# Ordering the experts of a mixture layer one step deeper and splitting the first half of the down product into three float32r matmuls

## What is computed

```
E, F, D, C = 64, 256, 512, 117          # experts, hidden width, token width, capacity of an expert
hg = einsum('ecd,efd->ecf', expert_in, w_gate)      # expert_in: the tokens routed to the expert, 117 slots
hu = einsum('ecd,efd->ecf', expert_in, w_up)
expert_out = einsum('ecf,edf->ecd', silu(hg) * hu, w_down)
sparse = segment_sum(gate * expert_out, token)      # each token chose 6 experts
```

## Time and profile before

| | before |
|---|---|
| median of 3 runs | 990.45 us (990.37 to 992.57) |
| the profiled execution, own time | 991.27 us |
| its span, first to last instruction | 989.4 us |
| TensorE busy | 912.4 us, 92% |
| VectorE, ScalarE, GpSimd busy | 71%, 45%, 38% |
| mean granted TensorE clock | 0.978 |
| moved by DMA | 159.73 MB |

### The profile page before, as it was taken

The page is one execution under the profiler, slowest core; times in us unless marked ns, Lnnn a source line. Parts: engine busy times, 40 slices in busy tenths (PEclk is TensorE's granted clock), DMA queues, the critical chain, the costliest instruction groups (busy, mean ns, idle before and its releaser), DMA issues. The chain is left out here.

```text
span 989.4 us, 13105 instructions
## 1 busy us (share of the span) xinstructions
PE 912.4 (92%) x4281; PEld 666.8 (67%) x4281; DVE 707.1 (71%) x1315; ACT 445.3 (45%) x696; POOL 380.6 (38%) x326
## 2 busy tenths in 40 slices
PE   5998999979999999989999989799999999999970
PEld 3997544448887778867788777566666666666640
DVE  6856789966654676777767888588677766677765
ACT  2665000052634535435264244566565666666630
POOL 2003000016600454105531153667766666766630
PEclk9999999979999999999999999999999999999995
DMA  6433000033200222012110263599999999999868
GB/s 176 145 121 122 18 1 0 0 117 128 86 1 7 89 86 86 1 54 85 52 61 11 74 224 128 161 331 325 339 340 354 349 329 355 357 356 325 285 176 204
DMA packets 57161, 159.73 MB, mean 161 GB/s; under 512 B 13901, under 2 KB 21651, under 8 KB 48656
## 3 DMA queue, kind: packets, MB, share of 16 engines
q1 hardware_dynamic: 44725, 147.50, 43.4%
q0 software_dynamic: 12288, 11.36, 4.2%
q10 hardware_dynamic: 91, 0.13, 0.1%
HBM read 152.71 MB, written 25.58 MB: 180 GB/s over the span
## 5 line engine op out<-in xcount | busy, mean ns | idle before, releaser
L259 PE MATMUL ps<-split_operands 128*125 128x512 f32 (+5 forms) x690 | 266.2, 386 | 16.2 <-DVE split_operands L1256 5.4
L260 PE MATMUL ps<-split_operands 128*125 128x512 f32 (+5 forms) x690 | 260.4, 377 | 0.0
L261 PE MATMUL ps<-split_operands 128*125 128x512 f32 (+5 forms) x690 | 260.1, 377 | 0.0
L653 POOL DMA_INDIRECT yrow_scratch<-work,row_i x64 | 151.6, 2369 | 95.4 <-ACT work L953 92.8
L259 PEld LDWEIGHTS ps<-split_operands 128*125 128x125 f32 (+3 forms) x690 | 129.5, 188 | 45.3 <-issue 9.6
L1470 DVE TENSOR_TENSOR gate_up_lo<-expert_weights,split_operands 128x2048 fp32r<-128x2048 f32 x64 | 147.0, 2297 | 0.5 <-ACT split_operands L935 0.5
L261 PEld LDWEIGHTS ps<-split_operands 128*125 128x125 f32 (+3 forms) x690 | 129.5, 188 | 26.5
L391 POOL TENSOR_TENSOR split_operands<-work,split_operands 128x512 fp32r<-128x512 f32 x66 | 83.5, 1293 | 162.0 <-ACT split_operands L373 153.1
L260 PEld LDWEIGHTS ps<-split_operands 128*125 128x125 f32 (+3 forms) x690 | 129.6, 188 | 23.6
L935 ACT ACTIVATE split_operands<-expert_weights 128x2048 fp32r<-128x2048 f32 x64 | 121.8, 1903 | 0.0
L1963 PE MATMUL ps<-expert_weights,work 128*117 128x512 f32 x256 | 120.3, 592 | 0.5 <-issue 0.5
(11 more groups left out here) (217 smaller groups left out, 1242.5 us busy)
## 6 DMA issues: line engine op xcount, KB each, us to landing
expert_weights<-experts_in SPq DMA_DIRECT2D x64, 1024.0 KB
expert_weights<-experts_in SPq DMA_DIRECT2D x64, 512.0 KB
work<-w_in SPq DMA_DIRECT2D x12, 1024.0 KB, 5.1
yrow_scratch<-work SPq DMA_DIRECT2D x5, 1500.0 KB
split_operands<-yrow_scratch SPq DMA_DIRECT2D x4, 1120.0 KB
work<-cw_in SPq DMA_DIRECT2D x3, 1024.0 KB, 5.2
work<-rows_in SPq DMA_DIRECT2D x10, 256.0 KB, 4.6
work<-wmix_in SPq DMA_DIRECT2D x4, 512.0 KB, 5.4
```

The source lines that it names most:

```text
L259: pe.matmul(o, a[1], b[0], start=start, stop=False)
L260: pe.matmul(o, a[0], b[1], start=False, stop=False)
L261: return pe.matmul(o, a[0], b[0], start=False, stop=stop)
L653: pool.indirect_dma_start(yrow, bass.IndirectOffsetOnAxis(ap=row_i[:, e:e + 1], axis=0), OS[e % 4], None, bounds_check=last_row, oob_is_er ...
```

## The change

The order on TensorE becomes gate_up(e), transpose_h(e - 1), transpose_x(e + 2), down(e - 2). The first half of the down product (the first 128 of 256 hidden values) becomes three float32r matmuls. So its weights need a high and a low part (`down_hi` on ScalarE and `down_lo` on VectorE, 128x512 each), and so do the turned hidden values (`h_part_hi` on ScalarE; in `h_part_lo` on VectorE a subtraction of 128x117 and a copy of 128x117 stand where one copy of 128x234 stood). The second half stays one plain float32 matmul. scale and with it scatter go one step later (scale(e - 2)). add_choice(0) goes behind the loop. Both engines' lists keep their other operations.

```diff
+        DN_hi = [rg(o, 512) for o in (16272, 32144)]
+        DN_lo = [sb(f"down_lo{r}", [P, 512], F32R, at=rg_at + 4 * (o + WA)) for r, o in enumerate(ring_at)]
...
+        HTP = sb("hidden_pairs", [P, 8 * CAP], F32R, at=fg_at + 4 * 4416)
+        HTR = [(HTP[:, cut(4 * CAP * i, 2 * CAP)], HTP[:, cut(4 * CAP * i + 2 * CAP, 2 * CAP)]) for i in range(2)]
...
+        def halves_done(e, down):
+
+            if down:
+                return len(plan) + min(2 * e + 4, E + e + 1)
+            return len(plan) + max(2 * e - 1, e + 1 if e < 2 else 0)
...
+            def down_hi(e):
+                act.wait_ge(S(f"load_in{RINGS + e % RINGS}"), 16 * (e // RINGS) + 16)
+                if e >= 2:
+                    act.wait_ge(S("o_ps"), e - 1)
+                act.activation(DN_hi[e % 2], RING[e % RINGS][:, cut(WA, 512)], ACT.Copy).then_inc(S("weight_hi"), 1)
+
+            def h_part_hi(e):
+                act.wait_ge(S("ht_ps"), NSH + e + 1)
+                if e >= 2:
+                    act.wait_ge(S("o_ps"), e - 1)
+                act.activation(HTR[e % 2][0][:, 0:CAP], ps[:, 4 + e % 2, 0:CAP], ACT.Copy).then_inc(S("ht_hi"), 1)
...
             for e in range(E):
                 silu(e)
+                if e >= 1:
+                    h_part_hi(e - 1)
                 if e + 2 < E:
                     gate_up_hi(e + 2)
-                if e >= 1:
-                    scale(e - 1)
+                if e >= 2:
+                    scale(e - 2)
+                down_hi(e)
                 if e + 2 < E:
                     xe_hi(e + 2)
+            h_part_hi(E - 1)
+            scale(E - 2)
             scale(E - 1)
...
-                dve.wait_ge(S("weight_hi"), len(plan) + e + 1)
+                dve.wait_ge(S("weight_hi"), halves_done(e, False))
...
-                dve.wait_ge(S("ht_ps"), NSH + e + 1)
+
+            def down_lo(e):
+                dve.wait_ge(S("weight_hi"), halves_done(e, True))
+                dve.tensor_tensor(DN_lo[e % RINGS][:], RING[e % RINGS][:, cut(WA, 512)], f(DN_hi[e % 2]), ALU.subtract).then_inc(S("weight_lo"), 1)
+
+            def h_part_lo(e):
+                dve.wait_ge(S("ht_hi"), NT * NL + e + 1)
                 if e >= 2:
                     dve.wait_ge(S("o_ps"), e - 1)
-                dve.tensor_copy(HTF[e % 2], ps[:, 4 + e % 2, 0:2 * CAP]).then_inc(S("ht_sb"), 1)
+                dve.tensor_copy(HTF[e % 2][:, CAP:2 * CAP], ps[:, 4 + e % 2, CAP:2 * CAP])
+                dve.tensor_tensor(HTR[e % 2][1][:, 0:CAP], ps[:, 4 + e % 2, 0:CAP], f(HTR[e % 2][0][:, 0:CAP]),
+                                  ALU.subtract).then_inc(S("ht_sb"), 1)
...
             for e in range(E):
                 gated(e)
+                if e >= 1:
+                    h_part_lo(e - 1)
                 if e + 2 < E:
                     gate_up_lo(e + 2)
+                down_lo(e)
+                if e + 2 < E:
                     xe_lo(e + 2)
+                if e == E - 1:
+                    h_part_lo(e)
                 if 2 <= e < 4 + TOPK:
                     gates(e - 2)
-                if e == E - 2:
-                    dve.wait_ge(S("shared_add"), NSH)
-                    add_choice(0)
-            for k in range(1, TOPK - 1):
+            dve.wait_ge(S("shared_add"), NSH)
+            for k in range(TOPK - 1):
                 add_choice(k)
...
-                for k in range(2):
-                    last = pe.matmul(ps[0:CAP, 6 + e % 2, :], HTF[e % 2][:, cut(k * CAP, CAP)], RING[e % RINGS][:, cut(WA + 512 * k, 512)],
-                                     start=(k == 0), stop=(k == 1))
+                pe.wait_ge(S("weight_lo"), halves_done(e, True))
+                mm3(ps[0:CAP, 6 + e % 2, :], sub(HTR[e % 2], A_, cut(0, CAP)), (DN_hi[e % 2], DN_lo[e % RINGS][:]), True, False)
+                last = pe.matmul(ps[0:CAP, 6 + e % 2, :], HTF[e % 2][:, CAP:2 * CAP], RING[e % RINGS][:, cut(WA + 512, 512)],
+                                 start=False, stop=True)
                 last.then_inc(S("o_ps"), 1)
...
             for e in range(E):
                 gate_up(e)
                 if e >= 1:
-                    down(e - 1)
-                transpose_h(e)
+                    transpose_h(e - 1)
                 if e + 2 < E:
                     transpose_x(e + 2)
+                if e >= 2:
+                    down(e - 2)
+            transpose_h(E - 1)
+            down(E - 2)
             down(E - 1)
```

More of the change, by code:

```diff
@@ L1948, in gate_up @@
             def gate_up(e):
-                pe.wait_ge(S("weight_lo"), len(plan) + e + 1)
+                pe.wait_ge(S("weight_lo"), halves_done(e, False))
                 pe.wait_ge(S("xe_lo"), e + 1)
```

## The result

The changed kernel takes 1003.75 us in the median of 20 runs (995.06 to 1010.14), the kernel before 997.65 on the same chip (20 runs, 989.39 to 1002.85). The ratio is 1.0067 with a 95% interval of 1.0041 to 1.0093: 0.7% slower, where 0.6% faster was forecast. (It is taken over the comparable runs and not from the two medians, which give 1.0061.) The profiled execution took 1008.2 with a span of 1005.4; the earlier trace rows are from one of 991.27.

The account below looks back on a forecast made before the run. TensorE, busy 92% of the span, was taken as the bound, with transfers next. Terms -9.9 - 0.8 + 0.4 + 1.0 + 3.5 = -5.8 us took the profiled 991.27 to 985.5, median 984.6 (0.6% less), range 981 to 990.

Parts of the forecast that it names:

- The step, -9.9: TensorE's loop step: three float32r matmuls replace one float32, 5.10 becomes 4.93 us over some 60 steps, -9.9 us.
- ScalarE, VectorE: Added loop operations: ScalarE rises to 4.3, VectorE to 4.1 to 4.6 us of 4.93; order and 1.0 us cover hide them.
- The +0.4 for the routing steps: Early loop steps with extra routing operations: VectorE runs over, TensorE waits about +0.4 us (between nothing and 2.5).
- The transfers, +1.0: Weight loads in the loop: 345 GB/s needed against 341 to 361 carried, last load slightly late, +1.0 us.
- The end, +3.5: Tail behind the last gate_up: scatters start later, moving the end by 1.8 to 5.7 us, taken as +3.5.
- The start, -0.8: Loop's start: the deeper order removes short idle waits of TensorE's transposes; half credited, -0.8 us.
- GpSimd locked out by VectorE: Rival in the loop: scatter and gather held by VectorE, step 5.6, 1024 us; weak form 992 to 1000; chance 0.10 together.
- The case with nothing left over: Rival: transfers carry 341 or less, tail 5.7 late, float32r switch costs 0.07; about 989.5 us; chance 0.18.

Follow-up runs that it names:

- e1_queue: Changed kernel with the gate and up load of expert e + 2 queued ahead of the down load of e: 993.68 us, ratio 0.9948.
- e5_before_late: Kernel before, with the down load, and with it the next gate and up load, released one step later: 1002.65 us, ratio 1.0047.
- e2_order: Kernel before with the deeper order on all engines and the plain float32 down product: 1003.26 us, ratio 1.0056.
- e9_pad: Changed kernel with 80 already satisfied SyncE waits behind each later down load: 994.55 us, ratio 0.996.
- e13_queue_one_spaced: e7_queue_one with 80 satisfied SyncE waits behind each down load, loads 2.81 us apart: 987.45 us, ratio 0.9919.
- e15_spaced_less: e13_queue_one_spaced with 27 waits in place of 80, loads 1.22 us apart: 994.19 us, ratio 0.9963.
- e14_late_paired: e7_queue_one with 80 satisfied SyncE waits ahead of each down load; loads stayed 0.38 us apart and went out no later: 995.25 us, ratio 0.996.
- e7_queue_one: Changed kernel with the gate and up load moved ahead by one expert only, still 0.37 us behind a down load: 998.8 us, ratio 1.0021.
- e12_mid: Changed kernel with the down product in the middle of gate_up, scale ahead of silu, and gate and up loads queued earlier: 1010.17 us, ratio 1.0127.
- e10_queue_pad: e1_queue with the same 80 satisfied SyncE waits as e9_pad: 990.74 us, ratio 0.993.

## Why the prediction was wrong, point by point

**The step, -9.9: right to 1 us.** It takes 4.94 to 4.95 against the forecast 4.93 (e1_queue has 53 steps of 4.945 on average), from 5.09 before: 0.15 saved in place of 0.166. The three float32r matmuls of the down product cost 0.23 each, and 0.07 more for the first, as forecast; gate_up behind a plain float32 matmul costs nothing extra.

**ScalarE, VectorE: right.** The added operations take 0.64 and 0.26, and 0.69 and twice 0.27. Neither engine holds TensorE when the loads are on time. The +0.4 for the routing steps did not come: silu(3) to silu(10) is 1.5 shorter, 1.0 of it the seven shorter steps.

**The transfers, +1.0: wrong, and the failed step.** I set the bytes a step needs against the rate of all engines together (343 to 361 GB/s), took 4.5 us for a load's own time, and found 8.7 us of margin. Between silu(10) and silu(63) the shorter step alone gives 262.1, which e1_queue shows; the changed kernel took 272.1. The term is +10. The rate was not what ran out: e1_queue draws 362 and 363 GB/s in the windows where the changed kernel draws 353 and 347. A load lands when its slowest engine does. When two loads go out 0.37 us apart that engine falls behind from load to load. The kernel before had it at 16.8 at the end of the loop and 18.6 of room, so it worked with 1.8 us to spare, and neither the waits nor the earlier trace rows show that; the change took 5.8 of that room. e5_before_late and e2_order show this without the split product, e9_pad, e13_queue_one_spaced and e15_spaced_less that the spacing governs it, and e14_late_paired that a busy SyncE doesn't. I had written that the loads go out a step later, and had set only their mean time against the room. One number of that working was off as well and changes nothing in it: 59 steps of 4.93 are 290.9 us and not 289.4, so the need is 343 GB/s, and at 341 the last load would be 1.8 late and not 3.3.
The Trainium skill has a line on this that I passed over: in DMA: Bandwidth & Descriptors, under Latency and other measured facts, two of the sixteen DMA engines are given as usually slower than the others, with a guess at the descriptor rings of the software path as the cause. The landings agree as far as the number goes: one engine is late in the changed kernel (DMA share 0.06 to 0.08 in the windows above), two in e7_queue_one. The loads here are of the hardware path, for which the Trainium skill gives no such ring; the gathers and scatters are of the software path. The cause was not tested. The Trainium skill gives no dependence on the spacing of loads, which here, together with a somewhat earlier issue, decides between 7.7 and 16.8 in the kernel before.

**The end, +3.5: right in kind, 1.1 too small.** It is 4.6, inside the 1.8 to 5.7 given; e2_order has 4.3 with the order alone, and e12_mid, whose scatters go out earlier, is shorter by 6.0.

**The start, -0.8: there only where the clock holds.** silu(0) to silu(3) is 0.2 longer in the changed kernel. Behind an idle time of 2.0 us in the second step its granted clock falls to 0.50 for 3.4 us, as it does in e1_queue, e9_pad, e10_queue_pad and e14_late_paired, which have 15.3 to 15.5. In e7_queue_one, e13_queue_one_spaced and e15_spaced_less it stays at 1.00 there, and they have 14.7, 14.7 and 14.2, which is 0.4 to 0.9 less than before. I had put no fall of the clock into this term.

**The rivals.** GpSimd locked out by VectorE did not happen: the scatter takes 2.43 as before. The case with nothing left over had the transfers in it, but at a lower total rate and at most 3.3 us; it put the kernel at 1.3 us less to 2.9 more than before, and the result is 6.1 more. None of my cases made the loads late at the same total rate.

**The sum.** By stages, forecast against measured: loop 10 to 63 -7.7 against +2.1, end +3.5 against +4.6, start -0.8 against +0.2, 3 to 10 -0.8 against -1.5. Of the 11.2 between the two sums the transfers have 9.0. With them mended, e1_queue has -7.9 - 1.5 + 0.4 + 3.3 = -5.7 and a measured 0.5% less. That this is the forecast's own sum is in part luck: the start is 1.2 worse than forecast, and the transfers, which cost nothing there, 1.0 better.

**The time itself.** The forecast 984.6 lies 19.2 below the measured 1003.75, and the change makes only 11.9 of that. The other 7.2 are the start: the three runs with the median of 990.45 were all at the faster level, and 20 runs have 997.65. Even a kernel without any change would have left the range of 981 to 990.

## What to carry to other kernels

Where a ring of loads runs near full rate, read the landing of the slowest engine against the time of use, load by load, and not the mean share or GB/s: a kernel can run with nearly all its margin spent (here 16.8 of 18.6 us) and show no wait. Releasing each load on its own event, some 2 us behind the one before, took a reordering of one queue here and gave 10 us. Read in the trace whether an added delay delays anything: two of the edits here fell into time that SyncE had free. A step on the compute side that moves a release moves the queue behind it; price that as room lost in front of the slowest landing.

## What the runs showed of the hardware that was not expected

When two loads are issued 0.37 us apart in one queue, again and again, one DMA engine in sixteen, and with enough room a second one, lands later and later: the last up to 20 us behind the issue, while the middle one stays at 5.5 to 8. With the loads 1.22 us apart the last reaches 16.8, 2.8 us apart 12.3. Which engine it is, and why it does not catch up, no run here shows. In the kernel before, with its step of 5.10, loads 1.7 and 3.4 us apart kept it level at 7.7.

The kernels have two levels of time, told apart by the mean granted clock. In the four sets of runs of the kernel before, those with a clock of 0.972 and above have a mean of 992.3 to 994.4 us, those below it 998.6 to 1000.1. In the profiled executions they part at one idle stretch of TensorE that ends between 573 and 578. It is 2.84 to 2.86 us long in thirteen of the fourteen (2.37 in e12_mid), and yet the clock stays at 1.00 in five and falls to 0.50 for 10 to 17 us in nine, from 1 us ahead of its end to 2 us behind it; the length of the idle stretch alone doesn't tell which. The median of a kernel depends on how many of its runs fall on either side: 3 of 20 at the higher level for the changed kernel, 2 of 12 for e1_queue, 5 of 8 for e13_queue_one_spaced. Differences of less than 0.5% between two medians are therefore not read as one kernel's merit here.
